# Squares, maximum and latent logits of the first unit put elsewhere in their queues (fused Perceiver layer)

## What is computed

```python
kv = jnp.concatenate([xn @ Wkv, ln @ Wkv], axis=1)
k = kv[:, :, 0].transpose(0, 2, 1, 3)
v = kv[:, :, 1].transpose(0, 2, 1, 3)
qn = rmsnorm(q, qn_g) * scale
kn = rmsnorm(k, kn_g)          # k over its norm per row and head
sim = jnp.einsum('bhid,bhjd->bhij', qn, kn)
attn = jax.nn.softmax(sim.astype(jnp.float32), axis=-1)
out = jnp.einsum('bhij,bhjd->bhid', attn, v)
```

## Time and profile before

| | us |
|---|---|
| median of three runs | 234.94 |
| the three runs | 234.29, 234.94, 234.95 |
| the profiled execution | 235.67 |
| its span, first to last instruction | 233.8 |

### The profile page before, as it was taken

The page is one execution under the profiler, slowest core; times in us unless marked ns, Lnnn a source line. Parts: engine busy times, 40 slices in busy tenths (PEclk is TensorE's granted clock), DMA queues, the critical chain, the costliest instruction groups (busy, mean ns, idle before and its releaser), DMA issues.

```text
span 233.8 us, 4163 instructions
## 1 busy us (share of the span) xinstructions
PE 222.3 (95%) x1443; PEld 193.1 (83%) x1443; DVE 152.3 (65%) x351; ACT 151.3 (65%) x331; POOL 79.5 (34%) x126
## 2 busy tenths in 40 slices
PE   7699999999989999999999999999999999899884
PEld 7366788887778989888898889899999988899773
DVE  1659999998887866867668655666766751304441
ACT  4335779998886869685767467787877755414151
POOL 5457867783383829263241500000000010000200
PEclk9999999999999999999999999999999999999999
DMA  6975111010000000000000799700000000000000
GB/s 168 288 240 202 45 31 43 22 48 22 0 22 3 0 6 0 0 0 3 0 0 0 252 412 331 184 0 3 1 3 0 0 1 3 0 3 0 0 3 22
DMA packets 11236, 13.80 MB, mean 59 GB/s; under 512 B 1584, under 2 KB 9936, under 8 KB 10960
## 3 DMA queue, kind: packets, MB, share of 16 engines
q1 hardware_dynamic: 10944, 13.01, 17.6%
q10 hardware_dynamic: 272, 0.52, 0.6%
HBM read 13.14 MB, written 0.13 MB: 57 GB/s over the span
## 4 chain that ended last, share of the span: by engine, by line
PE 65%; DVE 17%; ACT 5%; issue 4%; DMA 3%; POOL 3%; SPq 1%; ACTq 0%; POOLq 0%; DVEq 0%
PE banks L1222 18%; PE banks L1080 14%; PE banks L1132 8%; PE banks L1163 8%; PE banks L1354 5%; DVE small L823 4%; DVE sk L835 3%; DMA rows<-in_L_xattn_ln_x_b 3%; PE banks L1236 3%; PE banks L1165 2%; PE banks L1277 2%; ACT knT L570 2%; PE banks L1381 1%; ACT sk L553 1%; DVE sp L847 1%
## 5 line engine op out<-in xcount | busy, mean ns | idle before, releaser
L858 DVE TENSOR_TENSOR ptl<-banks,pth 128x512 fp32r<-128x512 f32 (+1 forms) x48 | 26.8, 558 | 24.3 <-ACT pth L606 23.2
L1222 PE MATMUL banks<-xnh,pth 128*128 128x256 f32 x128 | 37.6, 294 | 0.1
L1222 PE MATMUL banks<-xnh,ptl 128*128 128x256 f32 x128 | 36.2, 283 | 0.0
L1222 PE MATMUL banks<-xnl,pth 128*128 128x256 f32 x128 | 36.2, 283 | 0.0
L482 POOL TENSOR_TENSOR small<-small 128x16 f32<-128x16 f32 x7 | 20.4, 2915 | 32.1 <-DVE small L830 32.1
L553 ACT ACTIVATE sk<-banks 128x512 f32<-128x512 f32 x36 | 20.8, 604 | 15.4 <-PE banks L1132 15.0
L606 ACT ACTIVATE pth<-banks 128x512 fp32r<-128x512 f32 (+1 forms) x48 | 23.8, 495 | 10.6 <-PE banks L1080 9.5
L823 DVE TENSOR_REDUCE small<-sk 128x8 f32<-128x512 f32 x36 | 23.6, 679 | 7.3 <-ACT sk L553 7.3
L835 DVE TENSOR_TENSOR sk<-banks,small 128x512 f32<-128x512 f32 x36 | 23.0, 679 | 6.5 <-POOL small L482 6.5
L1080 PE MATMUL banks<-ident,sp 128*128 128x128 f32 x144 | 24.2, 279 | 1.0 <-ACT sp L587 0.9
L462 POOL COPY sp<-sp 128x64 f32<-128x64 f32 x16 | 3.8, 238 | 62.8 <-ACT sp L587 62.4
(11 more groups left out here) (183 smaller groups left out, 475.8 us busy)
## 6 DMA issues: line engine op xcount, KB each, us to landing
knT<-in_L_attn_qkv_kernel SPq DMA_DIRECT2D x1, 3072.0 KB, 12.0
raw<-in_ctx SPq DMA_DIRECT2D x16, 128.0 KB, 2.1
knT<-in_L_xattn_Wq SPq DMA_DIRECT2D x1, 1024.0 KB, 8.6
wv<-in_L_xattn_Wkv SPq DMA_DIRECT2D x1, 1024.0 KB, 5.3
wout_sb<-in_L_xattn_Wout SPq DMA_DIRECT2D x1, 1024.0 KB, 5.6
knT<-in_L_attn_out_kernel SPq DMA_DIRECT2D x1, 1024.0 KB, 14.5
wraw<-in_L_xattn_Wkv ACTq DMA_DIRECT2D x1, 512.0 KB, 4.2
wraw<-in_L_xattn_Wkv SPq DMA_DIRECT2D x1, 512.0 KB, 6.3
```

The lines of the kernel that those rows point to most:

```text
L858: nc.vector.tensor_tensor(ptl[:, j0:j1, :], banks[:, t3_bank(u, c), 0:(j1 - j0) * P].rearrange("p (j r) -> p j r", j=j1 - j0), pth[:, j0:j ...
L1222: nc.tensor.matmul(banks[:, u_bank(u), 0:D], p_[:, j, :], x_, start=(j == 0 and i == 0), stop=False)
```

## The change

Three pieces of order, all in unit 0. On ScalarE both `squares` of item 11 are taken out of the loop over units: half 0 now stands ahead of `exponentials(0)`, half 1 right behind it. On VectorE both sums and the clamp of item 11 stand ahead of `probs_low(0, 0)`, and `logits_max(1)` between `probs_low(0, 0)` and `probs_low(0, 1)`. On TensorE the third part of unit 1's logits follows the first two directly, ahead of `probs_transposed(0, 1)`, where it stood behind all transposes before. No instruction is added or dropped, and no wait is changed.

```diff
             nc.scalar.activation(warm[:, 1:2], warm[:, 0:1], ACT.Exp)
             unit_high(1)
+
+            squares(ITEMS_A + 1, 0)
             exponentials(0)
+            squares(ITEMS_A + 1, 1)
             for u in range(UNITS):
                 i = ITEMS_A + u
                 if u > 0:
                     mix_out(u - 1)
-                else:
-                    squares(i + 1, 0)
                 probs_high(u, 0)
...
                 if i < ITEMS:
                     keys_out(i, 0)
                     keys_out(i, 1)
-                if u == 0:
-                    squares(i + 1, 1)
-                elif i + 1 < ITEMS:
+                if u > 0 and i + 1 < ITEMS:
                     xt_high(tile(i + 1))
                 probs_high(u, 1)
...
                 if u == 0:
 
                     key_norm2(i + 1, 0)
-                    probs_low(u, 0)
                     key_norm2(i + 1, 1)
                     key_clamp(i + 1)
+                    probs_low(u, 0)
+                    logits_max(u + 1)
                     probs_low(u, 1)
-                    logits_max(u + 1)
                     probs_low(u, 2)
...
                 if u == 0:
                     probs_transposed(0, 0)
-                    logits(1, 0)
-                    logits(1, 1)
+                    for part in range(3):
+                        logits(1, part)
                     probs_transposed(0, 1)
                     probs_transposed(0, 2)
...
-                logits(u + 1, 2)
+                if u > 0:
+                    logits(u + 1, 2)
                 mix(u)
```

## The result

| | us | range or interval |
|---|---|---|
| before, median of 22 runs | 235.24 | 234.29 to 235.66 |
| changed, median of 22 runs | 234.87 | 233.82 to 235.54 |
| changed over before | 0.9981 | 95% interval 0.9972 to 0.999 |
| profiled execution, changed | 234.71 | span 232.8 |

The change makes the kernel 0.19% faster (0.1 to 0.28%), about 0.45 us. A second set of 12 runs of the same kernel on another occasion gave 0.9977 (0.9965 to 0.999).

The account below looks back on a forecast made before the run. TensorE, busy 95% of the span, was taken as the bound, so only unit 0's waits could give time. `exponentials(1)` moving from 67.62 to 67.24 us gains 0.38: 234.94 - 0.38 = 234.56, rounded 234.5 us; range 234.0 to 235.1 us.

Parts of the forecast that it names:

- First square hidden: ScalarE, between `kh` and `exponentials(0)`: half 0 takes 0.48 us in idle time, delay 0; 0.20 us late without overlap.
- Second square hidden: ScalarE, behind `exponentials(0)`: half 1 fits with 0.26 us to spare; nearly none of the 0.48 us removed later comes back.
- Maximum at 64.35 us on the old clock: VectorE: unit 1's maximum starts at 64.35 us instead of 66.30, ready at 65.6 instead of 67.5.
- What is late next: ScalarE: `exponentials(1)` waits behind unit 2's `kh` copy until 67.24 us, so 0.38 us gained of 1.9.
- The second chain: GpSimd's item 11 power starts 0.43 us earlier, `key_scale` at about 68.39 us; second key transposes in time by 0.06 us.
- The rule against it: VectorE's centering held by GpSimd's power to 68.35 us under the shared-port rule: net loss 0.2 us, 235.1 us; 2 in 100.
- The mix: TensorE, unit 0: starts where it did; its second third waits some 0.15 us less of 0.3, worth nothing by itself.
- Passed on to the end: From unit 1's first transposes on, each row stands 0.4 us earlier up to the kernel's end.
- Slower rival: ScalarE: first square without its input holds up unit 0's exponentials; +0.2 us, 235.15 us; 5 in 100.
- the cover for the early maximum: VectorE: the early maximum costs the second low third 1.2 us, covered by the first third of the mix.
- the early latent logits: TensorE: unit 1's 64-column logits matmul ahead of unit 0's second transposes delays `probs_high(0, 1)` by 0.07 us, between 0 and 0.3.

Follow-up runs that it names:

- The experiment with the exponentials first: Changed kernel with unit 1's exponentials ahead of the split of unit 2 on ScalarE; 0.9972 of the kernel before.

## Why the prediction was right

The forecast was 0.38 us gained. The profile has 0.40 to 0.42 us, and the time 0.19% or 0.45 us (0.24 to 0.66). The absolute 234.5 us is 0.37 us too low, 0.30 us of it because the median of before, 234.94 us from three runs, became 235.24 us over 22, and 0.06 us because I rounded 234.56 down.

- **First square hidden.** Right: 1.46 us from `kh` to exponentials, 1.45 before. Rows of one engine overlap by 0.1 us here as well.
- **Second square hidden**, and its removal from behind the key copies worth nothing there. Right: the second high third starts 4.05 us after unit 0's exponentials, and 3.97 before. The expected delay was 0.07 us and is 0.08.
- **Maximum at 64.35 us on the old clock**, 3.60 us after the exponentials. Right: 3.61. This was partly luck, since the clamp took 0.39 us in place of the 0.18 I used; the margins around it took that up.
- **What is late next.** Right, and the part that decided the size: the maximum came 1.94 us earlier and the exponentials 0.40, directly behind `kh`. The experiment with the exponentials first shows that it was `kh` (5.31 us).
- **The second chain.** The power starts 4.63 us after the exponentials (4.68 forecast), `key_scale` at 7.58 (7.64), and the eight key transposes take 1.06 us, not 1.14: the narrow margin held.
- **The rule against it.** The centering stood inside the power again (65.82, power from 64.83 us) and took 0.41 us. For other rows the rule does hold, see the last section.
- **The mix.** Half right, without consequence: I had it start where it did, and it starts 0.14 us later (4.07 us after unit 0's exponentials, 3.93 before). Its wait for the second low third fell away whole and not by half, so it ends 0.12 us earlier, inside the next wait of TensorE.
- **Passed on to the end.** Right: 0.42 us at the second transposes, 0.40 us at the last mix.
- **Slower rival.** It did not occur. Its condition was named rightly (a square without its input), and for the second square it costs what its input is late, 1.8 us.

What I had not seen is how much the pieces lean on each other. I wrote that the cover for the early maximum is the first third of the mix; that cover is 1.5 us long (64.27 to 65.78 us in the changed kernel) and holds only with the early latent logits, which I had booked as a loss of 0.07 us. Without them the gain is zero. And the part of the change that I priced as one of several, the squares, gives three quarters or more of it alone.

## What to carry to other kernels

When a wait is shortened, read on the waiting engine's own queue what stands directly ahead of the waiter: here a maximum that came 2 us earlier bought 0.4 us, because a 1.0 us copy stood there. Moving a blocking instruction ahead of another's input is two moves, its own and that of what it waits for, and they must be costed as one. And where a gain is a fifth of a per cent, measure distances between landmarks inside the profile, which repeated to 0.1 us here, while timed comparisons of one and the same kernel came out at 0.9966 and 0.9996.

## What the runs showed of the hardware

- A small `tensor_scalar` on VectorE (128 x 16, 0.17 to 0.18 us) took 0.39 and 0.72 us when a GpSimd `tensor_tensor` of 128 x 256 (an add or a subtraction) ran beside it, and ended within 0.03 us of that row's end; with the GpSimd row moved away it took 0.17 us again. The Trainium skill (SBUF — State Buffer, "Who interferes with whom") says that the engine that issues second is blocked for the other's whole instruction, and here the trace agrees.
- Beside GpSimd's power of 2.92 us the centering, a `tensor_scalar` of 128 x 256, took 0.40 to 0.41 us and was never held, so there the trace disagrees. It is not that the centering cannot be held: once in the first loop, in every profile, it took 0.80 or 0.81 us beside GpSimd's plain add. What differs between the two cases is the GpSimd row beside it; whether the power is free of the lock altogether or holds it for only a part of its time, no run separates. In the kernel before:

```profile
22.43 0.72 POOL L452 TENSOR_TENSOR xn<-xg,rows 128x256 f32<-128x256 f32 x1
```

```profile
22.50 0.80 DVE L791 TENSOR_SCALAR raw<-raw,small 128x256 f32<-128x256 f32 x1 [0.38 <-POOL small L429]
```

- In one profiled execution a wait of 2.3 us in TensorE's weight loads was followed, half a microsecond after they went on, by some 3 us at a granted clock of 0.50 to 0.61 (0.52 on average from 64.0 to 66.9 us). With idle matmuls in the wait the clock was 1.00. In the other profiles the waits of 0.2 to 0.8 us in units 0 and 1 were followed by no fall.
